# A second edge stage that picks destination logits in bfloat16 from three exact parts

## What is computed

```python
h = (x_flat @ W_gat).reshape(M, HEADS, NUM_EXPERTS)          # HEADS = NUM_EXPERTS = 4
a_src = (h * att_src).sum(-1)
a_dst = (h * att_dst).sum(-1)
e = jax.nn.leaky_relu(a_src[src] + a_dst[dst], negative_slope=0.2)
ee = jnp.exp(e - e_max[dst])
denom = jax.ops.segment_sum(ee, dst, num_segments=M)
agg = jax.ops.segment_sum(h[src] * (ee / denom[dst])[:, :, None], dst, num_segments=M)
...
hh = jax.nn.gelu(x @ W1[ei] + b1[ei], approximate=False)     # for each expert ei
out = out + g[..., None] * (hh @ W2[ei] + b2[ei])
```

## Time and profile before

| | us |
|---|---|
| median of 3 timed runs | 4169.92 (4165.97 to 4173.98) |
| span of the profiled execution | 5269.4 |
| PE busy in it | 3476.8 (66%) |
| DVE busy | 3039.4 (58%) |
| POOL busy | 2649.1 (50%) |
| ACT busy | 1492.7 (28%) |
| mean granted TensorE clock | 0.769 of full speed |

### The profile page before, as it was taken

How to read it: one execution, slowest core, us unless ns; L and a number is a source line. 1 busy time by engine, 2 the same in 40 slices (tenths; PEclk the granted TensorE clock), 3 DMA queues, 4 the chain that set the end, 5 groups by cost and what they waited for, 6 DMA issues and landing times. The chain is left out here.

```text
span 5269.4 us, 87248 instructions
## 1 busy us (share of the span) xinstructions
PE 3476.8 (66%) x16727; PEld 2890.9 (55%) x16728; DVE 3039.4 (58%) x9074; ACT 1492.7 (28%) x4965; POOL 2649.1 (50%) x2767
## 2 busy tenths in 40 slices
PE   5555555665566665666655537888888888888860
PEld 4444444444454444444444436777777777777760
DVE  5566655555565666666666665555555555555558
ACT  3222222222222222222222213333333333333310
POOL 1555555555555555555555522555555555555540
PEclk9777777777777777777777766888888888888865
DMA  5322333332333333333332242111111111111118
GB/s 121 82 78 75 84 82 81 84 84 79 82 82 99 101 101 102 100 101 101 101 84 78 77 79 49 20 20 22 20 20 22 20 20 22 20 21 21 20 16 239
DMA packets 224394, 356.43 MB, mean 68 GB/s; under 512 B 65743, under 2 KB 143761, under 8 KB 224051
## 3 DMA queue, kind: packets, MB, share of 16 engines
q0 software_dynamic: 114560, 234.67, 19.2%
q1 hardware_dynamic: 100624, 109.13, 7.5%
q10 hardware_dynamic: 8867, 9.05, 0.6%
HBM read 294.17 MB, written 45.66 MB: 64 GB/s over the span
## 5 line engine op out<-in xcount | busy, mean ns | idle before, releaser
L791 POOL DMA_INDIRECT msg<-table,idx x1680 | 1630.7, 971 | 1305.1 <-ACT rel L806 844.6
L1466 POOL DMA_INDIRECT xmsg<-xtable,xidx x1060 | 1002.8, 946 | 889.0 <-ACT xidx L1482 589.7
L1159 PE MATMUL psS_e<-msg,hot 128*125 128x260 f32 x3360 | 1182.9, 513 | 281.4 <-issue 162.2
L1159 PEld LDWEIGHTS psS_e<-msg,hot 128*125 128x125 f32 x3360 | 815.5, 254 | 512.3 <-issue 337.3
L888 DVE TENSOR_TENSOR room<-room,psS_e 125x260 f32 x842 | 356.5, 423 | 361.7 <-remote 180.9
L1024 DVE TENSOR_TENSOR msg<-msg,psW_e 128x1024 f32<-128x1024 f32 x420 | 509.5, 1213 | 8.8 <-issue 1.1
L812 ACT CAST hotT<-psT_e 125x512 bf16<-125x512 f32 x422 | 244.7, 580 | 951.6 <-remote 649.7
L1012 DVE TENSOR_REDUCE look<-psD_e 128x32 f32<-128x96 f32 x420 | 106.6, 254 | 700.7 <-remote 553.8
L1076 PE MATMUL psD_e<-ad_b,hotT 125*128 x1684 | 133.9, 182 | 559.8 <-issue 151.3
L1655 PE MATMUL psY<-w,hid 128*125 128x256 f32 x1600 | 457.1, 447 | 56.7 <-issue 29.6
L1065 PEld LDWEIGHTS psT_e<-ident,hot 128*125 128x125 f32 x1692 | 320.7, 240 | 248.2 <-ACT hotT L812 157.7
(11 more groups left out here) (308 smaller groups left out, 4436.9 us busy)
## 6 DMA issues: line engine op xcount, KB each, us to landing
msg<-table,idx POOLq DMA_INDIRECT x1680
experts_out<-y_room SPq DMA_DIRECT2D x101, 224.0 KB
y_back<-experts_out SPq DMA_DIRECT2D x25, 896.0 KB
xmsg<-xtable,xidx POOLq DMA_INDIRECT x1060
xs<-x_all SPq DMA_DIRECT2D x100, 125.0 KB
table<-hrow SPq DMA_DIRECT2D x50, 113.8 KB
x_all<-in_x SPq DMA_DIRECT2D x5, 1120.0 KB
xin<-in_x SPq DMA_DIRECT2D x50, 112.0 KB
```

Of the source, the lines that this page charges most:

```text
L791: nc.gpsimd.indirect_dma_start(msg[:, u, j, :], None, table[:, :], bass.IndirectOffsetOnAxis(ap=idx[:, u, j:j + 1], axis=0)).then_inc(gath ...
L1159: last = nc.tensor.matmul(psS[:, u % 2, j // GT, 0:ROW], hot[:, u, j, :], msg[:, u, j, :], start=j % GT == 0, stop=j % GT == GT - 1)
L1466: nc.gpsimd.indirect_dma_start(msg[:, u, j, :], None, xtable[:, :], bass.IndirectOffsetOnAxis(ap=idx[:, u, j:j + 1], axis=0)).then_inc(gat ...
```

## The change

```diff
-    CF = CB * 2 * XH
+    XP = 3 * 2 * XH
+    CF = CB * XP
...
-        hotT = sb("xhotT", [NB, 3, XT, P])
+        hotT = sb("xhotT", [NB, 3, XT, P], BF16)
+        xad_b = sb("xad_b", [NB, BLOCKS, 3, 2 * XH], BF16)
         hi = sb("xhi", [P, XT, CB])
-        prod = sb("xprod", [P, XT, CB, 2 * XH])
+        prod = sb("xprod", [P, XT, CB, XP])
...
+        xad_split = sem("xad_split")
...
             V.memset(acc[:], 0.0).then_inc(iotas_kept, 1)
+            left = prod[0:NB].rearrange("p j b f -> p (j b f)")[:, 0:BLOCKS * 2 * XH] \
+                .rearrange("p (b f) -> p b f", b=BLOCKS)
+            split = Chain(dve, xad_split)
+            split.link(V.tensor_copy(left, xad_all))
+            three_parts(nc, split, left, xad_b)
             dve.wait_ge(b2_loaded, 32)
...
                 V.tensor_tensor(prod[:], psD[:, 0:XT * CF].rearrange("p (j b f) -> p j b f", j=XT, b=CB),
-                                bcast(hi[:], 3, 2 * XH), ALU.mult).then_inc(picked_read, 1)
+                                bcast(hi[:], 3, XP), ALU.mult).then_inc(picked_read, 1)
                 dve.wait_ge(picked_read, k + 1)
-                ch.link(V.reduce_sum(look[:], prod[:].rearrange("p j b f -> p j f b"), AX_X))
+                ch.link(V.reduce_sum(look[:], prod[:].rearrange("p j b (s f) -> p j f (b s)", s=3), AX_X))
...
                     last = nc.tensor.matmul(psD[:, j * CF:(j + 1) * CF], hotT[:, TURN[w], j, :],
-                                            xad_all[:, bass.ds(c * CB, CB), :].rearrange("p b f -> p (b f)"),
+                                            xad_b[:, bass.ds(c * CB, CB)].rearrange("p b s f -> p (b s f)"),
                                             start=True, stop=True)
...
             turn(1, 1)
+            pe.wait_ge(xad_split, 6)
             pick(0, 0)
```

## The result

The changed kernel takes 4377.47 us (median of 4 runs, 4375.66 to 4380.02), the kernel before beside it 4171.76. The ratio is 1.049, 95% interval 1.0476 to 1.0505: 206 us slower.

What follows compares the result with a forecast made beforehand. The prediction took DVE's in-order chain in the second edge stage as the bound: 265 x (0.333 + 0.565) = +238 us, less 23 of waits, +215 on 4169.92 gives 4385 us, 5.2% slower; range 4320 to 4440, chance 0.70.

Steps and rivals of the forecast that it cites:

- the rival that asked for 133 us: Second edge stage: TensorE is the bound after all, so the stage gains 133 us, 4037 us; chance 0.06.
- DVE's trip of 56.7 us: Second edge stage, before the change: ten steps, 6 x 5.40 + 4 x 6.08 us, against TensorE's floor of 49.2.
- (a): DVE's product with the class mask, L1563: 160 elements become 480, 325 to 658 ns, +0.333 us a step.
- (b): DVE's reduction, L1566: 160 elements become 480 at the strided rate, 439 to 1004 ns, +0.565 us a step.
- the rival rate: DVE's reduction at the cheap 1.04 ns an element: 654 ns, total 4292 us; chance 0.17 shared with most waits swallowed.
- (c): TensorE's pick, L1624: float32 becomes one-pass bfloat16, 0.31 us, -0.5 us a step, off the path, worth nothing.
- (e): Once, ahead of the second edge stage: copy and three-part split on 400 elements, 3 us on DVE; nothing, up to +3.
- the cover: Stage start: pick 0 waits for ScalarE's first copy anyway, which was to hide the 3 us of splitting.
- The waits taken in: Second edge stage: the longer DVE step swallows waits for TensorE or ScalarE, half of 46 us idle, -23 us.
- the 120 us between the floors and the median: Whole kernel: summed floors of 4050 us against the timed median 4169.92; the stage's share by steps is 46 us.
- the rival that let the step take in all 120: Second edge stage: longer step swallows all 120 us as waits, +118, 4288 us; chance 0.17 shared with the cheap reduction.
- The clock: Rival: TensorE's granted clock falls and decides below 0.67; at 0.60 +425 us, 4595 us; chance 0.04.

Runs made afterwards that it cites:

- The run with the first part only: Kernel before with a bfloat16 pick of 40 columns using only the first of three parts, DVE's product and reduction unchanged: 4150.25 us, ratio 0.9956.
- the float32 run: Changed kernel with the table of parts and the turned one-hots in float32, so the pick takes two passes, DVE's work unchanged: 4382.6 us.

## Why the prediction was right

The forecast was 4385 us, slower, from +238 of DVE work less 23 of waits. The second profile of the kernel before and that of the changed one let each term be read. From the stage's first L1558 to its last (L1566 after the change), 1576.8 us became 1784.1. Split by the intervals between the starts of successive DVE operations, summed over the 264 steps:

```
interval                          before   changed   difference
reduction to first logit           130.4     282.2       +151.9
product to reduction                94.8     182.5        +87.7
one-hots to weighing               128.8      95.9        -32.9   (wait for the exponential)
wide to add                        118.3     105.8        -12.5   (wait for the sums)
second mask to product              98.9      96.4         -2.5   (wait for the pick)
last logit to one-hots             221.1     229.8         +8.7   (register load)
add to next mask                   307.7     315.3         +7.6   (register load, end of loop)
the others                                                 -0.7
sum                               1576.8    1784.1       +207.3
```

**The bound** was read right: DVE's chain in order, though the busy shares (TensorE 83%, DVE 53% in the earlier trace rows) pointed the other way. The run with the first part only, 20 us faster than the kernel before, and the float32 run, 5 us slower than the changed one, put a price on TensorE's saving of about 0.6 us a step; the rival that asked for 133 us fell. The sum behind the bound had a hole, though. DVE's trip of 56.7 us left out the end of the loop, which stands in the earlier trace rows as the 3.89 us ahead of their first L1558, and counted every even step as long as the first of a trip (5.39 us in the second profile, the bare ones 5.16). A trip by the medians above is 60.9 us. The order of the two engines is the same with either figure.

**(a) and (b), the two operations.** Forecast 0.333 + 0.565 = 0.898 us a step; measured 0.332 + 0.576 = 0.908 by the means, and 151.9 + 87.7 = 239.6 us by the intervals, for 238. The product came out at 657 ns for 658, the reduction at 1015 for 1004. The line through two strided reductions of other sizes was the right row to choose; the rival rate was right for another order in memory, where it gave 653 for 654. The sentence on 16-byte lines in the Trainium skill ("SBUF — State Buffer", Door 1: The DMA port swizzle) agrees with that pair, but it names no price: the prediction's words that the sum follows from this page alone are too strong, since the size came from the rows. The flat rate in the Trainium skill ("VectorE: DVE Perf Modes", The perf-mode tier table) fits the 653 ns over neighbours and not the 1015 ns.

**(c) the pick.** It takes 0.21 us for the assumed 0.31, off the path as said.

**(e) the split into parts.** The first L1558 began at 2446.5 us before and at 2450.3 after; the first product at 2452.8 and 2454.3. The product, which waits for the pick, came only 1.5 us later: the cover held for half of the 3 us.

**The waits taken in** were mis-sized. The prediction found 46 us of idle time in the stage and gave half of it. Measured, DVE's waits for the exponential and the sums were 47.5 us, and the longer step took in 45 of them, 47.9 by the intervals, the wait for the pick with them. The float32 run shows that the longer step does so by itself: without TensorE's saving these two waits are 0.8 us each. Half was a guess without a row, and that term was 22 to 25 us too small. That 46 lies so near to 47.5 is luck: it is a share of the 120 us between the floors and the median, of which some 80 us are the ends of the loop.

**What was left out** is +16.3 us in the intervals ahead of register loads. Two places in the loop hold most of it. In step 0 of a trip the interval from the last logit to the one-hots grew from 0.85 to 1.21 us, and at the end of step 3 the one from the add to the next mask grew from 0.79 to 1.15 (medians), 9 us each in 25 trips. The end of the loop grew by 0.14 us, and the same interval in steps 1, 5 and 7 shrank by 0.05 to 0.08. Both gaps stand at the same size in every version that makes the parts ahead of the stage, the two whose DVE work is that of the kernel before among them, and in neither version with the kernel before's table (the pick issued twice, and its own order changed). The instructions stand at other addresses where the setup is longer; whether that is the cause wasn't tried.

Together: 239.6 - 47.9 + 16.3 - 0.7 = 207.3, for a forecast of 215. With the later start (+3.8) and the stage's end (-0.7) the spans of the two profiles differ by 210.4 us; the timed medians differ by 206. The misses of 25 and 16 us have opposite signs, so it is in part luck that the sum lies within 9 us of the measurement.

**The reading of the profile before** was right in what it threw away, and wrong in one forecast. The 1100 us between that profile and the timed runs were waits of that one execution; the second profile of the same kernel is 4166.8 us long. The forecast that the changed kernel's profile would be 60 to 220 us longer than 5270 was wrong for the same reason: it was 4377.2. What disturbed that execution stays open. And most of the 120 us between the floors and the median is the loop's end, below, and no wait that a longer step could swallow: the rival that let the step take in all 120 had no room.

**The clock.** The granted clock fell from 0.92 to 0.86 in the stretch as TensorE's busy share fell from 91 to 77%, far from the 0.67 at which it would have decided.

## What to carry to other kernels

Ask which engine's instruction stream has no gaps, register loads included, not which one is busy the longest share: here an engine at 91% had room and one at 63% had almost none. Moving work from an engine with slack to the one that sets the step costs its price less the waits that it covers, here 240 us less 48; the same exact split into three parts is a small gain when TensorE accumulates them in PSUM, 4150.61 us, and a loss when DVE sums them, 4377.47. And lay out a table so that both the matmul's moving operand and DVE's reduction read neighbours: here that is worth 362 ns a step on DVE at 480 elements, and 69 ns a matmul on TensorE at 40 columns.

## What the runs showed of the hardware

The end of DVE's loop costs about 3 us a trip. In the second profile of the kernel before:

```profile
3229.69 0.26 DVE L1542 TENSOR_TENSOR acc<-acc,psS_g 125x100 f32 x1 [0.15 <-issue]
3233.92 0.23 DVE L1558 SCALAR_TENSOR_TENSOR xhi<-hi_all,cls_rel,psK 128x20 f32<-128x20 f32 x1 [3.98 <-issue]
```

In the middle of a trip this wait is some 0.5 us where it is 3.98 here. From DVE's branch to its next instruction pass 3.1 us in the median; for TensorE, ScalarE and GpSimd it is under 0.3. 25 trips make some 80 us, in both kernels. The Trainium skill ("Runtime: NRT & Kernel Launch", Instruction fetch mechanics) says that a taken branch to code outside the fetched window waits for a fetch. That the gap is such a fetch is not shown: no run here changed the loop's length.

A float32 reduction over elements 32 bytes apart in SBUF ran at 1.77 to 1.79 ns an element over a fixed 156 ns at 160 and 480 elements, and at 1.03 to 1.04 over neighbours. The first edge stage's reduction, with the same step of 32 bytes but from PSUM and three elements to a sum, takes 255 ns for 96 elements in the changed kernel, which lies on the cheap line (156 + 96 x 1.04 = 256; the dear one would give 326):

```profile
L1012 DVE TENSOR_REDUCE look<-psD_e 128x32 f32<-128x96 f32 x420 | 107.0, 255 | 210.8 <-DMA msg<-table,idx 150.3
```
